# Two passes of scores, their masks and the products with V in one half slot (layer 1 of a two-layer block, TensorE queue)

## The chip, the cores and the metric

The kernel runs on one core of a Trainium2 chip. The metric is the device time of one execution in microseconds. Before the change it is 2129.03 us, the median of three runs (2125.49, 2129.03 and 2129.18 us).

## The reference, cut to what matters

The program is two layers over x of shape (32, 256, 128), that is 32 sequences of 256 tokens. Each layer adds the outputs of an attention-like branch and a mixture of experts to its input. Layer 0 (a Mamba block and eight dense experts) is not touched. In layer 1, for each sequence:

```
q, k, v = up(x @ W_down)                    # 16 heads; q and k of 8 numbers per token, half of them rotated (rope)
scores  = einsum('bhqd,bhkd->bhqk', q, k) / sqrt(8);  causal mask to -inf
att     = softmax(scores);  y = einsum('bhqk,bhkd->bhqd', att, v);  x += y @ Wc
logits  = xn @ wg;  the two best of 128 experts per token, 32 places per expert
x      += g1 * expert(e1) + g2 * expert(e2)
```

## The kernel before, in words

`layer1` writes one queue of instructions per engine, all from the same clock of half slots. `schedule` (L1190 on) counts `now` from -24; a sequence has `HS1 = 12` half slots, and the tables `PE_AT`, `ACT_AT`, `DVE_AT`, `POOL_AT` and `SP_AT` (L1180 to L1184) say in which half slot, counted from the sequence's own start, a step is put into its engine's queue. So in the steady state each queue repeats every 12 half slots, and a step at 24 stands in half slot 0 of a later round. A half slot lasts no fixed time: it only orders the queues, which hold each other back by semaphores. Within one half slot the order is that of the statements in the engine's `half` function. The figures below are half slots modulo 12.

Attention goes over the 16 heads in six units u = 0 to 5. Units 0 and 3 hold four heads (of each half of the rows) with 128 columns each, the others two with 256. A unit passes through these steps:

- **First pass** (`first_pass`, L1358 on; matmuls at L1369 and L1376): scores into PSUM `S1`, and the causal mask added to them by four 64x64 matmuls (`diagonal`, L1355). VectorE then takes the row maxima out of `S1` (L1810). The next unit's first pass waits for that, since `S1` is there once. It stands in the even half slots, 2u.
- The negated maxima of all units are split into three bf16 parts (L1718 to L1724), transposed on TensorE (`nmt`, L1427), copied by ScalarE (`nm`, L1554) and sent by DMA through HBM into rows of `QS`.
- **Second pass** (`second_pass`, L1380 on; L1389 and L1396): transposed scores with the maxima subtracted, into PSUM `S2`, and the mask. ScalarE takes the exponential (L1569) into `PT`. The next unit's second pass waits for that, since `S2` is there once as well. It stands in the odd half slots, 17 + 2u.
- **Products with V** (`values`, L1411 and L1413), in four groups of heads, 128 rows by 9 columns each at four column positions, into PSUM `OT`; two copies (`osb`, L1563) take it away. They come last in their half slots but for `ot`, `yt` and `wc`.

Beside them TensorE has, per sequence: two transposes of normalised rows (`xnt`, L1433), projections for q and k (`qk`, L1439) and their rotated forms (`rot`, L1444), router logits (`g`, L1452), V (`v`, L1457), two running counts of the routing (`count`, L1466 and L1467), the map of places (`map`, L1473), and the epilogue (`ot` L1513, `yt` L1518, `wc` L1523). `xnt`, `qk`, `rot`, `g`, `v` and `nmt` share one PSUM bank `FR`: each waits until the one before it has been read. So `g` waits for VectorE's product `t2` (L1734), which reads what `rot` wrote, and `v` for the top-8 search (`top`, L1739 to L1742), which reads what `g` wrote. The counts share the bank `ACC` in the same way, with ScalarE's copies `cs` (L1550) as readers.

In ScalarE's queue the order within a half slot is xT, v, cs, nm, yT, osb, exp, spl; in VectorE's it is nms, t1, t2, top, mk, loc, oh, add, epi, x, and the maxima last.

The routing runs twice as fast for the first seven sequences (it then has a lead of seven), at one sequence per 12 half slots until it is done, and then the experts run in eight batches, every ten half slots, with indirect DMAs from POOL.

Of the kernel before, what the change touches and what calls it, by code (L numbers as in the profile page):

```python
# [13 lines left out]
P = 128  # L14
# [37 lines left out]
def layer0(nc, ctx, t, dram, scratch):  # L52
# [321 lines left out]
    def _(pe):  # L374
# [93 lines left out]
        def fore(h, n, q):  # L468
            if h == PE_AT["xqt"]:

# [550 lines left out]
GROUPS = 4  # L1021
HG = HEADS // GROUPS
# [6 lines left out]
UNITS = 6  # L1029
# [45 lines left out]
def layer1(nc, ctx, t, dram, scratch, out):  # L1075
# [32 lines left out]
    wc = sb("wc", [P, D])  # L1108
    cos = sb("cos", [P, L]); sin = sb("sin", [P, L])
    maskq = sb("maskq", [P, HG, 64], BF16); maskk = sb("maskk", [P, HG, 64], BF16)  # L1110
# [21 lines left out]
    S1 = ctx.enter_context(nc.psum_tensor("S1", [P, 2, 512], F32))  # L1132
    S2 = ctx.enter_context(nc.psum_tensor("S2", [P, 2, 512], F32))
# [43 lines left out]
    parts_d, nm_d, xn_d, y_d = scratch["parts"], scratch["nm"], scratch["xn"], scratch["y"]  # L1177
    FEW = 4 * J1

    PE_AT = dict(xnt=-21, g=-17, count=(-13, -10), map=-3, qk=-20, rot=-18, v=-3, p1=0, nmt=12, p2=17, pv=(21, 24, 26, 30), ot=(32, 35), yt=36, wc=40)  # L1180
    ACT_AT = dict(xT=-20, cs=(-12, -9), v=-1, spl=(-15, -12), nm=13, exp=18, osb=(26, 32), yT=39)
    DVE_AT = dict(top=-15, mk=-13, loc=(-11, -8), oh=-8, add=-2, t1=-18, t2=-15, mx=1, nms=12, epi=(35, 36), x=43)
    POOL_AT = dict(norm=-23, keep=-13, val=-5, qk=-14, r1=-14, spl=-10)
    SP_AT = dict(xn=-14, parts=(-13, -9, -8), load=-5, nm=12, nm_in=14, we=-16)  # L1184
# [136 lines left out]
    def _(pe):  # L1321
# [26 lines left out]
        def diagonal(scores, mask, heads, off):  # L1348


            for r in range(2):
                for c in range(2):
                    x = 64 * (c ^ r)
                    out = scores[64 * c:64 * c + 64, r, :].rearrange("p (j k) -> p j k", j=heads)[:, :, off + 64 * c:off + 64 * c + 64]
                    last = nc.tensor.matmul(out, identb[x:x + 64, x:x + 64], mask[x:x + 64, 0:heads, :], start=False, stop=True, tile_position=(x, 64 * c))  # L1355
            return last

        def first_pass(u, n, m):  # L1358
            S, a = u // 3, u % 3
            if u == 0:  # L1360
                if n == 0:
                    pe.wait_ge(loaded, LOADED)
                pe.wait_ge(parts_in.sem, parts_in.at(n, 64))
            pe.wait_ge(max_done.sem, max_done.at(n, u))
            if a == 0:
                for j in range(HG):
                    for r in range(2):
                        q, k = QS[rows(r, KQ + 2), m, 4 * S + j, 0:P], KS[rows(r, KQ + 2), m, 4 * S + j, 0:P]
                        nc.tensor.matmul(S1[:, r, j * P:(j + 1) * P], q, k, start=(j == 0), stop=False, tile_position=(64 * r, 0))  # L1369
                last = diagonal(S1, maskq, HG, 0)  # L1370
            else:
                for j in range(2):
                    for r in range(2):
                        i = 4 * S + 2 * (a - 1) + j
                        q, k = QS[rows(r, KQ + 2), m, i, P:L], KS[rows(r, KQ + 2), m, i, :]
                        nc.tensor.matmul(S1[:, r, j * L:(j + 1) * L], q, k, start=(j == 0), stop=False, tile_position=(64 * r, 0))  # L1376
                last = diagonal(S1, maskq, 2, P)
            last.then_inc(p1.sem, 1)

        def second_pass(u, n, m):  # L1380
            S, a = u // 3, u % 3
            if u == 0:
                pe.wait_ge(nm_in.sem, nm_in.at(n, 32))
            pe.wait_ge(exp_done.sem, exp_done.at(n, u))
            if a == 0:
                for j in range(HG):
                    for r in range(2):
                        k, q = KS[rows(r, KQ + 5), m, 4 * S + j, P:L], QS[rows(r, KQ + 5), m, 4 * S + j, P:L]
                        nc.tensor.matmul(S2[:, r, j * P:(j + 1) * P], k, q, start=(j == 0), stop=False, tile_position=(64 * r, 0))  # L1389
                last = diagonal(S2, maskk, HG, 0)  # L1390
            else:
                for j in range(2):
                    for r in range(2):
                        i = 4 * S + 2 * (a - 1) + j
                        k, q = KS[rows(r, KQ + 5), m, i, 0:P], QS[rows(r, KQ + 5), m, i, :]
                        nc.tensor.matmul(S2[:, r, j * L:(j + 1) * L], k, q, start=(j == 0), stop=False, tile_position=(64 * r, 0))  # L1396
                last = diagonal(S2, maskk, 2, 0)
            last.then_inc(p2.sem, 1)

        def values(g, n, m):  # L1400
            S, b = g // 2, g % 2
            if g == 0:
                pe.wait_ge(v_done.sem, v_done.at(n, 1))
                pe.wait_ge(ot_copied.sem, ot_copied.at(n - 1, 2))
            elif g == 2:
                pe.wait_ge(ot_copied.sem, ot_copied.at(n, 1))
            pe.wait_ge(exp_done.sem, exp_done.at(n, 3 * S + b + 2))
            for j in range(HG):
                r, e = j // 2, j % 2
                head, out = 8 * r + 2 * g + e, slice(32 * j, 32 * j + DH + 1)  # L1410
                nc.tensor.matmul(OT[out, b, :], V[m][:, 0, head, :], PT[:, S, 1 + b, 512 * r + L * e:512 * r + L * e + L],  # L1411
                                 start=True, stop=False, tile_position=(0, 32 * j))
                last = nc.tensor.matmul(OT[out, b, P:L], V[m][:, 1, head, :], PT[:, S, 0, 512 * r + P * (2 * b + e):512 * r + P * (2 * b + e + 1)],  # L1413
                                        start=False, stop=True, tile_position=(0, 32 * j))
            last.then_inc(pv.sem, 1)

        def half(due, ahead, now):
            for u in range(UNITS):
                for n, m in due(PE_AT["p1"] + 2 * u):
                    first_pass(u, n, m)  # L1420
                for n, m in due(PE_AT["p2"] + 2 * u):
                    second_pass(u, n, m)
            for n, m in due(PE_AT["nmt"]):
                pe.wait_ge(nm_step.sem, nm_step.at(n, 4))
                front_free("nmt", n)
                for j in range(J1):
                    last = nc.tensor.transpose(FRb[:, j * P:(j + 1) * P], NMS[:, j, :, :].rearrange("p r h -> p (r h)"), identb[:])  # L1427
                last.then_inc(fr_nm.sem, 1)
            for n, m in ahead(PE_AT["xnt"]):
                pe.wait_ge(xn_ready.sem, xn_ready.at(n, 2))  # L1430
                front_free("xnt", n)
                for j in range(J1):
                    last = nc.tensor.transpose(FR[:, j * P:(j + 1) * P], XN[:, m, j, 0:D], ident[:])  # L1433
                last.then_inc(fr_x.sem, 1)
            for n, m in due(PE_AT["qk"]):
                pe.wait_ge(xT_done.sem, xT_done.at(n, 1))
                front_free("qk", n)
                for q, w in enumerate((wq, wk)):
                    last = nc.tensor.matmul(FR[:, q * L:(q + 1) * L], w[:], xnT[:, n % RING, :], start=True, stop=True)  # L1439
                last.then_inc(fr_qk.sem, 1)  # L1440
            for n, m in due(PE_AT["rot"]):
                front_free("rot", n)
                for q, w in enumerate((wqr, wkr)):
                    last = nc.tensor.matmul(FR[:, q * L:(q + 1) * L], w[:], xnT[:, n % RING, :], start=True, stop=True)  # L1444
# [49 lines left out]
            for b in batch(7, now):  # L1494
# [4 lines left out]
                        last = nc.tensor.matmul(ACC[32 * j:32 * j + 32, k * P:(k + 1) * P], XGT[:, k, 32 * j:32 * j + 32], WE[:, b % WBUF, 4 * k + j, :],  # L1499
                                                start=True, stop=True, tile_position=(0, 32 * j))  # L1500
                last.then_inc(applied, 1)
            for g in range(GROUPS):
                for n, m in due(PE_AT["pv"][g]):
                    values(g, n, m)
            for j in range(J1):
                for n, m in due(PE_AT["ot"][j]):
                    if j == 0:
# [400 lines left out]
```

## Time and profile before

| | |
|---|---|
| median of the runs | 2129.03 us |
| profiled execution: span from first to last instruction | 2167.2 us (no other time of it is shown) |
| PE, DVE, ACT, POOL busy | 1941.7, 1681.5, 1340.8, 1310.3 us |
| PE, share of the span | 90% |
| layer 1 | from about 1477 us to the end |
| mean granted TensorE clock | 0.943 of full speed |

The profile is one execution; its engines' rows carry the line of the kernel that issued the instruction. A matmul's end is modelled, so the time from one start to the next is used below rather than its duration. "idle before <-X" names what ended the idle time ahead of an instruction.

### The profile page before, as it was taken

The page shows a single profiled execution, that of the slowest core. Times are in us where ns is not written, and L with a number is a line of the kernel's source. Part 1 is how long each engine was busy: PE and PEld are TensorE (multiplying, and loading weights), DVE is VectorE, ACT ScalarE, POOL GpSimd, SP SyncE. Part 2 cuts the span into 40 slices and gives each one's busy share as a digit, 9 for nine tenths or more (in the row PEclk, how much of TensorE's full clock was granted, in tenths as well). Part 3 has the DMA queues.
Part 4 walks back from the last instruction along what each step waited for, and adds up shares of the span by engine and source line. Part 5 has one row for each costly group of instructions (what it writes and reads, how often), then busy time and mean ns, then how long its engine had stood idle before and what let it go on. Part 6 is the DMA issues. An engine that isn't in the chain of part 4 may idle for free. (4 is left out here: it accounts for less than half of the span.)

```text
span 2167.2 us, 41765 instructions
## 1 busy us (share of the span) xinstructions
PE 1941.7 (90%) x14386; PEld 1129.5 (52%) x14386; DVE 1681.5 (78%) x2731; ACT 1340.8 (62%) x2423; POOL 1310.3 (60%) x1005
## 2 busy tenths in 40 slices
PE   5789999999999999999999999957999999988775
PEld 3455555555555555555555555534555555554442
DVE  5689888888798888887988888857888877774345
ACT  3677676776776777767767777631555555544343
POOL 2586886877867778778687787744433333325430
PEclk7999999999999999999999999976999999998787
DMA  8632633515425335154153362316444444454438
GB/s 205 145 93 56 137 81 80 136 36 124 105 47 134 84 75 138 39 120 112 43 137 84 70 136 66 82 45 174 120 115 123 116 114 116 118 155 129 119 95 239
DMA packets 212029, 235.27 MB, mean 109 GB/s; under 512 B 31590, under 2 KB 150414, under 8 KB 207694
## 3 DMA queue, kind: packets, MB, share of 16 engines
q1 hardware_dynamic: 207116, 227.98, 42.2%
q0 software_dynamic: 2048, 4.18, 0.7%
q8 instruction: 126, 2.06, 0.4%
q14 instruction: 99, 0.81, 0.1%
q10 hardware_dynamic: 2640, 0.24, 0.1%
HBM read 165.51 MB, written 66.85 MB: 107 GB/s over the span
## 5 line engine op out<-in xcount | busy, mean ns | idle before, releaser
L733 POOL TENSOR_TENSOR dBx<-REP,BC 128x1024 f32<-128x1024 f32 x256 | 604.2, 2362 | 260.1 <-DVE dA L906 227.7
L906 DVE TENSOR_TENSOR_SCAN dA<-dA,dBx 128x512 f32<-128x512 f32 x512 | 626.5, 1224 | 151.9 <-POOL dBx L733 105.8
L405 PE MATMUL UP<-xnT,W 128*128 128x512 f32 x1024 | 524.3, 631 | 56.7 <-ACT hT L607 43.4
L414 PEld LDWEIGHTS DN<-W,hT 128*128 128x128 f32 x4096 | 469.3, 192 | 99.4 <-issue 88.2
L414 PE MATMUL DN<-W,hT 128*128 128x128 f32 x4096 | 495.7, 278 | 0.3 <-ACT GD L614 0.3
L598 ACT ACTIVATE dA<-REP,A 128x512 f32<-128x512 f32 x512 | 354.2, 695 | 86.9 <-DVE PR L915 78.7
L607 ACT ACTIVATE hT<-UP,b 128x512 f32<-128x512 f32 x512 | 355.5, 694 | 78.6 <-PE UP L405 70.7
L915 DVE TENSOR_TENSOR PR<-dA,BC 128x512 f32<-128x512 f32 x512 | 353.6, 691 | 33.7 <-DVE dA L906 21.0
L405 PEld LDWEIGHTS UP<-xnT,W 128*128 128x128 f32 x1024 | 180.3, 195 | 296.6 <-issue 150.5
L1810 DVE TENSOR_REDUCE NM<-S 128x4 f32<-128x1024 f32 (+1 forms) x192 | 234.1, 1219 | 128.1 <-PE S L1355 76.8
L1569 ACT ACTIVATE PT<-S 128x1024 f32<-128x1024 f32 x192 | 197.1, 1026 | 124.5 <-PE S L1355 94.5
L614 ACT ACTIVATE GD<-DN,gate 128x128 f32<-128x128 f32 x512 | 145.8, 367 | 129.7 <-PE DN L414 128.5
L743 POOL TENSOR_TENSOR FF<-FF,GD 128x512 f32<-128x512 f32 x128 | 163.2, 1275 | 6.1 <-ACT GD L614 6.1
L426 PE MATMUL YS<-PR,fold 128*32 128x512 f32 x1024 | 141.8, 627 | 1.3 <-DVE y L921 0.7
L1623 POOL TENSOR_TENSOR t<-t 128x512 f32<-128x512 f32 x32 | 40.7, 1272 | 152.6 <-DVE t L1734 152.6
L1411 PE MATMUL OT<-PT,V 128*9 128x256 f32 x1024 | 87.7, 398 | 11.3 <-ACT PT L1569 7.9
L1550 ACT COPY CS<-ACC 128x256 f32<-128x256 f32 x64 | 23.8, 373 | 102.8 <-PE ACC L1467 102.8
L1629 POOL TENSOR_TENSOR SPL<-t,SPL 128x512 bf16<-128x512 f32 x32 | 37.1, 1160 | 79.3 <-ACT SPL L1575 79.3
L1563 ACT COPY OSB<-OT 128x512 f32<-128x512 f32 x64 | 37.5, 586 | 69.7 <-PE OT L1413 57.0
L426 PEld LDWEIGHTS YS<-PR,fold 128*32 128x32 f32 x1024 | 20.6, 110 | 106.8 <-issue 73.1
L972 DVE SCALAR_TENSOR_TENSOR xch<-FRO,convw,xch 128x510 f32<-128x510 f32 (+2 forms) x93 | 69.2, 744 | 8.6 <-ACT xch L657 6.4
L1376 PE MATMUL S<-KS,QS 50*128 50x256 bf16 x512 | 52.8, 285 | 13.4 <-DVE NM L1810 11.0
(251 smaller groups left out, 2667.1 us busy)
## 6 DMA issues: line engine op xcount, KB each, us to landing
BC<-s_b SPq DMA_DIRECT2D x128, 256.0 KB, 6.2
REP<-s_dx SPq DMA_DIRECT2D x124, 256.0 KB, 7.5
REP<-s_delta SPq DMA_DIRECT2D x124, 256.0 KB, 8.8
s_parts<-SPL SPq DMA_DIRECT2D x64, 192.0 KB
KS<-s_parts SPq DMA_DIRECT2D x64, 192.0 KB
QS<-s_parts SPq DMA_DIRECT2D x64, 192.0 KB
s_dx<-tz SPq DMA_DIRECT2D x16, 512.0 KB, 3.1
s_y<-zeros SPq DMA_DIRECT2D x32, 256.0 KB, 2.9
```

What stands on the lines that cost most here:

```text
L405: nc.tensor.matmul(UP[k % 2][:], W1[:, e % E0, f * P:(f + 1) * P], xnT[:, q, :], start=True, stop=True).then_inc(upf.sem, 1)
L414: last = nc.tensor.matmul(DN[:, j * P:(j + 1) * P], hT[:, e % 2, f, j * P:(j + 1) * P], W2[:, e, f, :], start=(f == 0), stop=(f == FB - 1))
L426: last = nc.tensor.matmul(YS[CB * j:CB * j + CB, :], fold[:], PR[:, (DB * b + j) % (2 * DB), :], start=(q == 0), stop=(q == NQ - 1), tile_ ...
L598: nc.scalar.activation(dA[:, k % 3, :], DR[:, h, j, :], ACT.Exp, scale=A[:, h, j, q:q + 1]).then_inc(da_ready.sem, 1)
L607: nc.scalar.activation(hT[:, e % 2, f, :], UP[k % 2][:], ACT.Relu, bias=b1[:, e % E0, f:f + 1]).then_inc(relu_done.sem, 1)
L614: last = nc.scalar.activation(GD[:, e % 2, j, :], DN[:, j * P:(j + 1) * P], ACT.Copy, scale=gate[:, par, j, e:e + 1])
L733: nc.gpsimd.tensor_tensor(dBx[:, s % 2], DX[:, h, j:j + 2, :], BC[:, q // 2, q % 2, :].unsqueeze(1).to_broadcast([P, 2, T0]), ALU.mult).th ...
L743: nc.gpsimd.tensor_tensor(FF[:, par], FF[:, par], GD[:, e % 2], ALU.add).then_inc(acc_done.sem, 1)
L906: nc.vector.tensor_tensor_scan(h, h, dBx[:, k // 2 % 2, k % 2, :], 0.0, ALU.mult, ALU.add).then_inc(scan_done.sem, 1)
L915: nc.vector.tensor_tensor(PR[:, k % (2 * DB), :], dA[:, k % 3, :], BC[:, q // 2, 2 + q % 2, :], ALU.mult).then_inc(prod_done.sem, 1)
L1569: nc.scalar.activation(PT[:, u // 3, u % 3, :], S2[:].rearrange("p b w -> p (b w)"), ACT.Exp, scale=SCALE).then_inc(exp_done.sem, 1)
L1810: nc.vector.tensor_reduce(NM[:, 0 if a == 0 else 1, :].rearrange("p (r i) -> p r i", r=2)[:, :, heads], S1[:].rearrange("p r (j k) -> p r ...
```

## The change

In layer 1 the masks are taken out of `first_pass` and `second_pass` into `first_mask` and `second_mask`, which also carry the signals to VectorE and ScalarE. TensorE's half slot now begins with the scores of both passes, then both masks, then the products with V; all else follows. The second pass moves by one half slot, from 17 + 2u to 18 + 2u, so that it falls into the same even half slots as the first. The exponentials move with it (18 to 19), the products from (21, 24, 26, 30) to (22, 24, 28, 30), and the copies `osb` from (26, 32) to (25, 31). Durations, sizes and numbers of instructions stay.

```diff
-    PE_AT = dict(xnt=-21, g=-17, count=(-13, -10), map=-3, qk=-20, rot=-18, v=-3, p1=0, nmt=12, p2=17, pv=(21, 24, 26, 30), ot=(32, 35), yt=36, wc=40)
-    ACT_AT = dict(xT=-20, cs=(-12, -9), v=-1, spl=(-15, -12), nm=13, exp=18, osb=(26, 32), yT=39)
+    PE_AT = dict(xnt=-21, g=-17, count=(-13, -10), map=-3, qk=-20, rot=-18, v=-3, p1=0, nmt=12, p2=18, pv=(22, 24, 28, 30), ot=(32, 35), yt=36, wc=40)
+    ACT_AT = dict(xT=-20, cs=(-12, -9), v=-1, spl=(-15, -12), nm=13, exp=19, osb=(25, 31), yT=39)
...
-                last = diagonal(S1, maskq, HG, 0)
...
-                last = diagonal(S1, maskq, 2, P)
-            last.then_inc(p1.sem, 1)
+        def first_mask(u):
+            (diagonal(S1, maskq, HG, 0) if u % 3 == 0 else diagonal(S1, maskq, 2, P)).then_inc(p1.sem, 1)
...
+        def second_mask(u):
+            (diagonal(S2, maskk, HG, 0) if u % 3 == 0 else diagonal(S2, maskk, 2, 0)).then_inc(p2.sem, 1)
...
             for u in range(UNITS):
                 for n, m in due(PE_AT["p1"] + 2 * u):
                     first_pass(u, n, m)
+            for u in range(UNITS):
                 for n, m in due(PE_AT["p2"] + 2 * u):
                     second_pass(u, n, m)
+            for u in range(UNITS):
+                for n, m in due(PE_AT["p1"] + 2 * u):
+                    first_mask(u)
+            for u in range(UNITS):
+                for n, m in due(PE_AT["p2"] + 2 * u):
+                    second_mask(u)
+            for g in range(GROUPS):
+                for n, m in due(PE_AT["pv"][g]):
+                    values(g, n, m)
             for n, m in due(PE_AT["nmt"]):
...
-            for g in range(GROUPS):
-                for n, m in due(PE_AT["pv"][g]):
-                    values(g, n, m)
```

TensorE's queue over 12 half slots, after the change (s1, s2 scores, m1, m2 masks, with the unit): 0: s1(0) s2(3) m1 m2 values(1) nmt yt. 2: s1(1) s2(4) m1 m2 count1. 3: xnt. 4: s1(2) s2(5) m1 m2 values(2) qk wc. 6: s1(3) s2(0) m1 m2 values(3) rot. 7: g. 8: s1(4) s2(1) m1 m2 ot0. 9: v map. 10: s1(5) s2(2) m1 m2 values(0). 11: count0 ot1. Half slots 1 and 5 are empty there.

ScalarE's: 0: cs0 spl1. 1: nm osb0 exp(3). 3: cs1 yT exp(4). 4: xT. 5: exp(5). 7: osb1 exp(0). 9: exp(1) spl0. 11: v exp(2). Before, exp(3) stood in 0, exp(4) in 2 behind osb0, exp(5) in 4, exp(0) in 6, exp(1) in 8 and exp(2) in 10.

## Rows read from the trace of the kernel before

**Rows 1.** Windows: busy time (instructions) of PE, PEld, DVE, ACT, POOL; clock, DMA.

```profile
1650.00:1700.00 50.00, 48.34 (x629) 28.96 (x625) 40.17 (x100) 28.28 (x46) 18.22 (x21) 1.00 0.45 119
...
1950.00:2000.00 50.00, 44.06 (x549) 25.14 (x547) 23.68 (x46) 23.96 (x45) 24.51 (x24) 0.83 0.47 130
```

**Rows 2.** Chain that ended last: start, us, what; `qk` of sequences 0, 4, 6, 23.

```profile
1494.34 2.01 PE FR L1439 x4
...
1575.08 1.06 PE FR L1439 x4
...
1616.01 1.06 PE FR L1439 x4
...
1913.02 1.06 PE FR L1439 x4
```

**Rows 3.** Timeline of a steady round: start, us, engine, line, operation, count, [idle].

```profile
1700.69 0.60 PE L1467 MATMUL ACC<-CS,last_row 128*128 128x256 f32 x2
...
1701.33 0.37 ACT L1550 COPY CS<-ACC 128x256 f32<-128x256 f32 x1 [0.40 <-PE ACC L1467]
1701.60 0.38 ACT L1558 COPY yT<-EP 128x256 f32<-128x256 f32 x1
...
1703.51 0.67 PE L1439 MATMUL FR<-xnT,wq 128*128 128x256 f32 x2
...
1704.99 0.40 PE L1389 MATMUL S<-QS,KS 53*128 53x128 bf16 x8
...
1706.11 0.70 PE L1444 MATMUL FR<-xnT,wqr 128*128 128x256 f32 x2
...
1707.17 0.64 PE L1411 MATMUL OT<-PT,V 128*9 128x256 f32 x8
1707.37 0.68 DVE L1734 TENSOR_TENSOR t<-FR,sin 128x512 f32<-128x512 f32 x1
...
1707.96 0.39 PE L1396 MATMUL S<-QS,KS 53*128 53x256 bf16 x4
1708.12 0.59 ACT L1563 COPY OSB<-OT 128x512 f32<-128x512 f32 x1 [1.43 <-PE OT L1413]
...
1708.28 0.25 PE L1355 MATMUL S<-maskk,identb 64*64 64x128 bf16 x4
1708.46 0.71 PE L1452 MATMUL FR<-wvg,xnT 128*128 128x128 f32 x4
1708.61 1.03 ACT L1569 ACTIVATE PT<-S 128x1024 f32<-128x1024 f32 x1
...
1709.21 0.50 DVE L1739 MAX8 mx<-FR 128x8 f32<-128x128 f32 x2 [1.16 <-PE FR L1452]
...
1710.30 1.20 DVE L1810 TENSOR_REDUCE NM<-S 128x4 f32<-128x1024 f32 x1
...
1713.26 1.22 DVE L1810 TENSOR_REDUCE NM<-S 128x4 f32<-128x1024 f32 x1
...
1715.42 0.28 PE L1427 MATMUL FR<-identb,NMS 128*128 128x128 bf16 x2 [0.16 <-DVE NMS L1724]
...
1715.77 0.37 ACT L1554 COPY NMT<-FR 48x256 bf16<-48x256 bf16 x1
...
1716.30 1.22 DVE L1810 TENSOR_REDUCE NM<-S 128x8 f32<-128x1024 f32 x1
...
1717.58 0.39 PE L1376 MATMUL S<-KS,QS 50*128 50x256 bf16 x4 [0.22 <-DVE NM L1810]
```

**Rows 4.** Timeline, earlier, while the routing runs at double pace.

```profile
1581.30 0.68 PE L1452 MATMUL FR<-wvg,xnT 128*128 128x128 f32 x4 [0.58 <-DVE t L1734]
```

**Rows 5.** Waits from 1930 to 2090 us: total us, times, longest us.

```profile
DVE NM L1810 <- remote: 43.9, 11, 6.7
```

**Rows 6.** Timeline, late: a gap on PE, and the projection that follows.

```profile
1983.04 0.22 PE L1355 MATMUL S<-maskq,identb 64*64 64x128 bf16 x1 [1.02 <-issue]
...
1985.44 1.22 PE L1439 MATMUL FR<-xnT,wq 128*128 128x256 f32 x2
```

More of the change, by code:

```diff
@@ L1389, in second_pass @@
                         nc.tensor.matmul(S2[:, r, j * P:(j + 1) * P], k, q, start=(j == 0), stop=False, tile_position=(64 * r, 0))
-                last = diagonal(S2, maskk, HG, 0)
             else:
@@ L1396, in second_pass @@
                         nc.tensor.matmul(S2[:, r, j * L:(j + 1) * L], k, q, start=(j == 0), stop=False, tile_position=(64 * r, 0))
-                last = diagonal(S2, maskk, 2, 0)
-            last.then_inc(p2.sem, 1)
+        def second_mask(u):
+            (diagonal(S2, maskk, HG, 0) if u % 3 == 0 else diagonal(S2, maskk, 2, 0)).then_inc(p2.sem, 1)
         def values(g, n, m):
```

## The prediction

> **What bounds the kernel now.** I read the windows first, to see which engine is full in layer 1, then the chain of waits for the pace of a sequence, then the timeline of one steady round. In the steady part PE is busy 48.34 of 50 us at full clock, VectorE 40.17 and ScalarE 28.28 [rows 1]: TensorE's queue sets the pace. Between the projections of sequences 6 and 23 lie 297.0 us, so a round takes 17.5 us; between 0 and 6 it is 20.3 us, while the routing runs at double pace, and from 23 on rounds are longer and uneven [rows 2, 5]. The reader is to see in the timeline that PE goes from one group to the next almost without waiting, and that PE's busy time holds gaps that no semaphore explains: from a pass of scores to its mask 0.32 us (1707.96 to 1708.28) for 512 columns in two pairs, which at 2.4 GHz are 0.213 us, and from the mask to `g` 0.18 us for 128 columns, 0.053 us [rows 3]. So each change between arrangements (64-row scores, 64x64 masks, 32-column products, whole array) costs 0.11 to 0.13 us.
>
> **What the change removes.** Counting changes of arrangement in TensorE's queue over a round: 38 before (5, 2, 4, 3, 3, 2, 4, 3, 3, 4, 2, 3 by half slot) and 22 after (4, 3, 4, 4, 3, 4 by pair). That is 16 fewer at 0.12 us, 1.9 us of PE time a round; PE alone would need 15.6 us. Neither number of matmuls nor their columns change. Bounds for one saved change: 0 (the cost stays in each group) and 0.127.
> The Trainium skill, page "TensorEngine Tiling (Array Packing)", section "Key Properties", says that changing the tiling mode drains the engine while moving between tiles does not. By that rule the gaps above are drains, and the trace agrees (0.11 and 0.13 us). By that rule alone a round would fall to 15.6 us; that is a rival below.
>
> **What it adds: waits.** Before, one pass stood in each half slot, so PE had the other pass and some projection to do while VectorE or ScalarE read `S1` or `S2`. Afterwards both passes stand at the head of the even half slot, and the odd ones hold little or nothing. I lay one steady round after the change, from the start of the first pass of unit 0 at 0.00, by intervals of [rows 3] between starts.
> 1. Two passes of scores take 0.32 + 0.21 us (the second without a change of arrangement; bound above 0.32), both masks 0.18 + 0.05, and 0.05 more for each mask of four heads: products 1 start at 0.87. These take 0.79 (1707.17 to 1707.96): `nmt` at 1.66.
> 2. ScalarE's half slot 1 is nm, osb0, exp(3), in order. nm starts 0.35 after `nmt` (1715.42 to 1715.77), at 2.01; a copy of this size frees ScalarE after 0.27 (1701.33 to 1701.60), osb after 0.49 (1708.12 to 1708.61); so exp(3) starts at 2.77 and ends at 3.80. Its input was masked already near 0.8. The second pass of unit 4 starts at 3.86 (0.06 for a release, as from 1716.30 + 1.22 to 1717.58), where PE would have come to it near 2.4. First wait: 1.5 us. Before, exp(3) stood ahead of nm and osb0.
> 3. In the next half slots the order is cs1, yT, exp(4), and cs1 waits for `count1`, which now follows both masks. From the second pass, 0.32 + 0.18 + 0.05 + 0.12 (the count's first product, 256 columns) brings L1467 to 4.53; the copy follows 0.64 later (1700.69 to 1701.33), at 5.17; yT and two copies' time put exp(4) at 5.71 and the second pass of unit 5 at 6.80. PE would have been there near 5.7. Second wait: about 1.1 us. The maxima of unit 1 (4.5 to 5.7) are not later than that.
> 4. Scores and masks 0.55, products 2 0.79: `qk` at 8.14; `qk` with `wc` 1.48 (1703.51 to 1704.99): first pass of unit 3 at 9.62. Again 0.87 and 0.79: `rot` at 11.28.
> 5. `g` must wait for t2, since both use `FR`. t2 starts 1.26 after `rot` (1706.11 to 1707.37) and takes 0.68: `g` at 13.30, where `rot` alone would end at 12.3. Third wait: 1.0 us. Before, products 3 and the second pass of unit 1 stood between `rot` and `g`; both have moved ahead of them. That this wait exists when the cover is short is seen earlier in the kernel, where `g` stood 0.58 us for t2 [rows 4].
> 6. `g` to the top-8 search 0.75, from there to the maxima of unit 4 1.09, from these to those of unit 5 2.96 (add, mk and the epilogue lie between), 1.23 and 0.06 to release the next round: 19.39. PE comes there at about 19.2, so VectorE ends the round narrowly.
>
> So a round takes 19.4 us in place of 17.5, PE's saved 1.9 us having turned into idle time: 3.8 us between what PE needs and the round, in the three waits and some smaller ones. Queued behind PE's waiting instruction is all its later work, first masks and maxima among it; that is in the sum. DMAs don't move: SP and POOL keep their places. The load of `QS` and `KS` keeps its lead of five half slots, and the second pass of unit 0, which needs the maxima by DMA, comes 7.6 us after nm (9.62 against 2.01); before it was 6.7 (1715.77 to 1704.99 + 17.5).
>
> **The sum.** Steady: 17 rounds by 1.9 = +32 us (bounds 1.5 and 2.3 a round, as the release and the second pass of scores vary: 26 to 39). First six rounds: in the later ones a round takes 20.5 us (1575.08 to 1616.01, two rounds) [rows 2]; PE has 3.0 us more there, which fills part of the waits, while the double routing adds searches and copies of its own; an estimate of 1.1 each, +7 (bounds 0 and 1.9, 0 to 11). The end, from 1913 us: VectorE alone stood 43.9 us there for something that the trace can't name [rows 5], and these delays don't depend on the order. Without routing the chain above loses the copy cs1 and the wait for t2 before `g`; I take half a microsecond by eight rounds, +4 (0 to 9). Clock: PE would be busy some 80% of a round, about half between 2.2 and 6.8. Late in the trace a gap of 1.02 us was followed by projections at 1.2 GHz: 1.22 us for a wq product where 0.67 is usual [rows 3, 6]. Step 4 holds 2.8 us of PE work on the path, which doubles at worst to add 2 us or a little more. The ends are no fall at all and one in every round, 0 and 34; the rows show only that a gap of this size can do it, so I stay near the lower end: a quarter of the 17 rounds at 2 us, +8. Together 32 + 7 + 4 + 8 = +51 us. The profiled execution spans 2167.2 us, 38 more than the median of the runs; on it this makes 2218, and as the steady rounds are bound by queues and not by the recording I add the same 51 to the median: 2180 us.
>
> **Rivals.**
> - Faster: PE stays the bound and the saved changes pay. For it: PE is at 97% and the gaps are there to be saved. Against it: it needs exp(3) to reach unit 4 before PE does, at 2.4 rather than 3.86, and `g` not to meet t2. It decides at those two places. 23 rounds by 1.9 less and about 5 at the end: 2129 - 49 = 2080 us. Chance 0.12.
> - No change or little: two of the three waits are shorter than laid out, say because copies release sooner or PE's groups shrink more than by 0.12 a change; 1.9 us saved against 2 us waited. 2130 us, 2115 to 2150. Chance 0.12.
> - The clock: with 20% of PE idle the granted clock falls in most rounds, as in the late window, 0.83 at 44 of 50 us busy [rows 1]. Then 17 rounds by 2 us instead of a quarter of them: 2180 + 26 = 2206, 2195 to 2235. Chance 0.20.
> - The change doesn't do what it says: the two passes are queued together but changes cost the same. Then at most 16 by 0.12 come back on the path, 17 rounds by 1.9: 2180 to 2212 us. Its chance is held in the forecast's and the clock's, whose ranges cover it.
>
> **How the numbers follow.** Forecast 2180 us with its own range 2150 to 2205, chance 0.56. Faster rival 0.12, little change 0.12, clock 0.20. From 2130 to 2218 lie the forecast, half of the little-change case and most of the clock's: about 0.8. A measurement of this kernel tells 0.2%, some 4 us, from no change: faster 0.14 (the first rival and a sixth of the second), same 0.05, slower 0.81.
>
> **What would show it.** PE's share in the steady windows falls from 97% to near 80%; the round grows to about 19.4 us. Step 2: the second-pass matmuls at the old L1396 idle about 0.5 us and more on the exponential, once right after osb. Step 3: the same again, with ScalarE waiting for the count. Step 5: `g` idles 1.0 us on t2 once a round. The saving: score to score near 0.21 us without a gap. Wrong would be rounds under 17.5 us, no idle time at `g`, or an exponential that starts ahead of osb0.

## The result, and the profile after

The changed kernel takes 2205.95 us, the median of four runs (2204.43 to 2208.63 us), beside 2129.05 us for the kernel before: a ratio of 1.0374, 95% interval 1.0358 to 1.0391. That is 77 us slower, 26 us above the forecast of 2180: 1 us over the forecast's own range of 2150 to 2205, and inside the 2130 to 2218 that the prediction gave about 0.8. In the kernel after, most of layer 1's lines stand nine to twelve lower: `qk` is L1451, `g` L1464, t2 L1743, the maxima L1819, the exponential L1578, the passes L1369/L1375 (first) and L1390/L1396 (second).

The spans of the two profiled executions, 2167.2 and 2202.6 us, differ by only 35, since the profiled execution of before lay 38 above its own median. Its end is the long part: 254 us from its last projection of [rows 2], against 223 after and 211 to 232 in every other kernel profiled here. So the stages below are compared up to there.

The projections that answer to [rows 2], from the chain of waits of the kernel after (start, us):

```profile
1490.02 2.00 PE FR L1451 x4
...
1578.37 1.06 PE FR L1451 x4
...
1624.20 2.00 PE FR L1451 x4
...
1979.69 1.80 PE FR L1451 x4
```

(In both kernels two projections, of sequences 0 and 1, stand ahead of the first row; the rows called 0, 4, 6 and 23 are of sequences 2, 6, 8 and 25. The intervals are not touched by this. The first projection of layer 1 starts at 1453.3 us in the kernel before, so layer 1 begins earlier than the 1477 us named ahead.) The first six rounds take 134.2 us in place of 121.7, the 17 after them 355.5 in place of 297.0. So 71 of the 77 us are in these 23 rounds.

The window that answers to the first of [rows 1] (busy time and instructions of PE, PEld, DVE, ACT, POOL; clock; DMA), and PE's waits from 1620 to 1920 us, 14 rounds (us in total, times, longest us):

```profile
1650.00:1700.00 50.00, 39.38 (x555) 24.65 (x555) 39.76 (x93) 24.09 (x41) 17.35 (x20) 1.00 0.36 98
```

```profile
PE S L1375 <- DVE NM L1819: 26.3, 40, 1.2
...
PE FR L1464 <- DVE t L1743: 12.2, 14, 0.9
PE S L1396 <- ACT PT L1578: 8.8, 14, 0.7
PE S L1369 <- DVE NM L1819: 7.8, 14, 0.6
```

The reader is to see that PE is busy 79% of the steady window where it was 97%, at full clock, and that in every round it waits four times for maxima, once for t2 and once for an exponential. An undisturbed round is 20.19 us. One of them, from the timeline (start, us, engine, line, operation, count, [idle]):

```profile
1709.08 0.70 PE L1456 MATMUL FR<-xnT,wqr 128*128 128x256 f32 x2
...
1710.24 0.69 DVE L1743 TENSOR_TENSOR t<-FR,sin 128x512 f32<-128x512 f32 x1 [0.71 <-PE FR L1456]
...
1711.08 0.68 PE L1464 MATMUL FR<-wvg,xnT 128*128 128x128 f32 x4 [0.87 <-DVE t L1743]
1711.69 0.39 PE L1375 MATMUL S<-KS,QS 50*128 50x256 bf16 x4
1711.80 0.50 DVE L1748 MAX8 mx<-FR 128x8 f32<-128x128 f32 x2 [0.87 <-PE FR L1464]
1711.92 0.38 PE L1396 MATMUL S<-QS,KS 53*128 53x256 bf16 x4
...
1712.88 1.21 DVE L1819 TENSOR_REDUCE NM<-S 128x4 f32<-128x1024 f32 x1
...
1714.20 1.17 POOL L1635 TENSOR_TENSOR t<-t,SPL 128x512 f32<-128x512 f32 x1 [1.93 <-ACT SPL L1584]
...
1714.39 1.53 DVE L1757 TENSOR_TENSOR MK<-iota,ef 128x512 bf16<-128x512 f32 x1
...
1716.34 1.21 DVE L1819 TENSOR_REDUCE NM<-S 128x4 f32<-128x1024 f32 x1
...
1717.70 0.40 PE L1369 MATMUL S<-KS,QS 50*128 50x128 bf16 x8 [0.56 <-DVE NM L1819]
1717.70 1.16 POOL L1638 TENSOR_TENSOR SPL<-t,SPL 128x512 bf16<-128x512 f32 x1 [0.46 <-ACT SPL L1584]
1717.80 1.11 DVE L1729 TENSOR_TENSOR NR<-NM,NMS 128x32 f32<-128x32 f32 x1
...
1718.59 0.64 PE L1413 MATMUL OT<-PT,V 128*9 128x256 f32 x8
...
1719.41 0.29 PE L1439 MATMUL FR<-identb,NMS 128*128 128x128 bf16 x2
...
1720.00 0.58 ACT L1572 COPY OSB<-OT 128x512 f32<-128x512 f32 x1
...
1720.29 1.22 DVE L1819 TENSOR_REDUCE NM<-S 128x8 f32<-128x1024 f32 x1
1720.48 1.02 ACT L1578 ACTIVATE PT<-S 128x1024 f32<-128x1024 f32 x1
1721.57 0.39 PE L1375 MATMUL S<-KS,QS 50*128 50x256 bf16 x4 [1.23 <-DVE NM L1819]
...
1723.10 0.37 ACT L1559 COPY CS<-ACC 128x256 f32<-128x256 f32 x1 [1.60 <-PE ACC L1479]
...
1723.63 1.04 ACT L1578 ACTIVATE PT<-S 128x1024 f32<-128x1024 f32 x1
1723.69 0.39 PE L1375 MATMUL S<-KS,QS 50*128 50x256 bf16 x4 [0.41 <-DVE NM L1819]
...
1724.73 0.39 PE L1396 MATMUL S<-QS,KS 53*128 53x256 bf16 x4 [0.65 <-ACT PT L1578]
...
1726.07 0.70 PE L1451 MATMUL FR<-xnT,wq 128*128 128x256 f32 x2
...
1727.58 0.40 PE L1369 MATMUL S<-KS,QS 50*128 50x128 bf16 x8
```

Two things are to be seen. PE waits at all the places that the prediction laid by hand, though at the first of them (1721.57) the row names maxima and not an exponential. And two VectorE instructions are longer than before: MK (the mask of the chosen experts), 1.53 us at 1714.39, and NR (the rest of the maxima after their first bf16 part), 1.11 us at 1717.80. Each starts 0.1 to 0.2 us behind a GpSimd instruction (1714.20, 1717.70) and ends only after it. In the kernel before they last (1640 to 1900 us; count | busy us, mean ns of one | idle):

```profile
L1748 DVE TENSOR_TENSOR MK<-iota,ef 128x512 bf16<-128x512 f32 x15 | 10.4, 693 | 0.5
L1720 DVE TENSOR_TENSOR NR<-NM,NMS 128x32 f32<-128x32 f32 x15 | 2.9, 192 | 0.5
```

### The profile page after: what moved, and what is told of

It is laid out like the page before. It is cut to its first block and busy times, and to the rows that moved or that the text cites. A ratio compares the mean times of both kernels' runs of the same rounds, so it can differ in the third digit from the quotient of the medians.

```text
span 2202.6 us, 41765 instructions
## 1 busy us (share of the span) xinstructions
PE 1904.2 (86%) x14386; PEld 1124.4 (51%) x14386; DVE 1717.5 (78%) x2731; ACT 1335.0 (61%) x2423; POOL 1309.3 (59%) x1005
## 5 line engine op out<-in xcount | busy, mean ns | idle before, releaser
L405 PE MATMUL UP<-xnT,W 128*128 128x512 f32 x1024 | 517.5, 623 | 59.3 <-ACT hT L607 44.8
L1819 DVE TENSOR_REDUCE NM<-S 128x4 f32<-128x1024 f32 (+1 forms) x192 | 233.9, 1218 | 82.9 <-PE S L1355 82.7
L1578 ACT ACTIVATE PT<-S 128x1024 f32<-128x1024 f32 x192 | 197.2, 1027 | 88.9 <-PE S L1355 88.6
L1375 PE MATMUL S<-KS,QS 50*128 50x256 bf16 x512 | 54.0, 292 | 51.6 <-DVE NM L1819 51.3
L1647 POOL TENSOR_TENSOR OV<-OH,VAL 128x256 bf16<-128x256 bf16 x32 | 20.2, 630 | 111.4 <-DVE OH L1770 98.8
L1396 PE MATMUL S<-QS,KS 53*128 53x256 bf16 x512 | 53.0, 287 | 24.7 <-ACT PT L1578 24.4
```

The lines of the kernel that those rows point to most:

```text
L405: nc.tensor.matmul(UP[k % 2][:], W1[:, e % E0, f * P:(f + 1) * P], xnT[:, q, :], start=True, stop=True).then_inc(upf.sem, 1)
L1578: nc.scalar.activation(PT[:, u // 3, u % 3, :], S2[:].rearrange("p b w -> p (b w)"), ACT.Exp, scale=SCALE).then_inc(exp_done.sem, 1)
L1819: nc.vector.tensor_reduce(NM[:, 0 if a == 0 else 1, :].rearrange("p (r i) -> p r i", r=2)[:, :, heads], S1[:].rearrange("p r (j k) -> p r ...
```

## The experiments

Round lengths below are from one `qk` to the next in the steady stretch of each profile; "undisturbed" is the value that repeats at full clock. Ratios are to the kernel before, run beside each. Of the tables' lines the diffs show only the entries that differ; what stands behind # in them is a note.

**One cause undone at a time.** First, the products with V back at their old place in the half slot, so that `g` finds cover again (out from ahead of `nmt`, in ahead of `ot`):

```diff
-            for g in range(GROUPS):
-                for n, m in due(PE_AT["pv"][g]):
-                    values(g, n, m)
...
+            for g in range(GROUPS):
+                for n, m in due(PE_AT["pv"][g]):
+                    values(g, n, m)
```

> The changed kernel with the products with V back at their old place in the half slot, behind the projections and counts; all else as changed. Theory (waits): products 3 stand between rot and g again, so g's idle time on t2 (0.87 us a round in the changed kernel) falls under 0.2 us; against that the products of group 1 come behind nmt, which delays osb0 and the exponential of unit 3 by some 0.3 us, and three more changes of arrangement cost 0.3: the round goes from 20.2 to 19.6 to 19.8 us, the time to 2194 to 2200 us. Rival (g's wait is harmless, or another wait takes its place at once): round within 0.1 of 20.2, time 2203 to 2209.

2214.01 us, ratio 1.0428 [1.0406, 1.0450]; undisturbed round 19.98. A miss: `g` no longer waits (the list of PE's waits doesn't hold it), but the second pass now waits 16.7 us in 260 for exponentials, and `nmt` 14.6, for a VectorE cast that has grown to 1.07 us. So the wait for t2 was real, but with it gone the undisturbed round is only 0.2 us shorter, since two others took its place; and MK fell back to 693 ns there, so the 0.2 is not the worth of that wait alone. The time rose all the same, as the lower clock took more of it: the granted clock from 1640 to 1900 us is 0.91, where the changed kernel has 0.95, and the 17 steady rounds take 361.6 us, where they took 355.5.

The copies `osb` back at (26, 32), so that exp(3) no longer stands behind one:

```diff
-osb=(25, 31)
+osb=(26, 32)
```

> The changed kernel with the copies osb back at half slots 26 and 32, so that the exponential of unit 3 stands ahead of osb0 and behind nm only. Theory from the trace after: the second pass of unit 4 would be free 0.5 us earlier, but the first pass of unit 1 ahead of it in the queue waits for the maxima of unit 0 until 3.87 us of the round, so nothing comes of it: round 20.1 to 20.2, time 2202 to 2208 us. Rival (step 2 of the prediction as written: the exponential behind osb0 sets the first wait): 0.5 us less a round, 19.7, time 2194 to 2199 us.

2194.43 us, 1.0332 [1.0312, 1.0352]; undisturbed round 20.20, unchanged. The first pass of unit 1 holds the queue ahead of the second pass of unit 4, and it waits for maxima, not for exp(3). The time fell in part because fewer rounds ran at the lower clock, five of 17 and not eight: the 17 take 349.8 us in place of 355.5. The rest of the 11.5 us lies mostly behind them, where the profile's end takes 211.7 us in place of 223.0; what made that shorter is not shown.

ScalarE's casts for the split of q and k later, so that GpSimd's L1635 and L1638 move off MK and NR:

```diff
-spl=(-15, -12), nm=13
+spl=(-13, -11), nm=13
```

> The changed kernel with ScalarE's two casts spl, which release POOL's r1 and spl subtractions, moved from -15 and -12 to -13 and -11 half slots. Theory: VectorE's MK (1.53 us against 0.69 before) and NR (1.11 against 0.19) are stretched because they run while POOL runs a tensor_tensor; moved, MK falls to 0.7 and NR to 0.2, the maxima of unit 5 come 0.5 us earlier and those of unit 0 0.9 us: round 19.4 to 19.6, time 2191 to 2196 us. Rival (the stretch belongs to these instructions' own operands or to PE's traffic): durations stay at 1.1 and 1.5, time 2203 to 2209 us.

2199.67 us, 1.0342 [1.0315, 1.0369]; undisturbed round 19.66. VectorE's instructions between 1640 and 1900 us, of after and then of this kernel (count | busy us, mean ns of one | idle):

```profile
L1757 DVE TENSOR_TENSOR MK<-iota,ef 128x512 bf16<-128x512 f32 x12 | 18.4, 1531 | 0.4
L1729 DVE TENSOR_TENSOR NR<-NM,NMS 128x32 f32<-128x32 f32 x12 | 13.3, 1109 | 0.4
...
L1727 DVE CAST NMS<-NM 128x32 bf16<-128x32 f32 x12 | 2.2, 181 | 0.4
```

```profile
L1727 DVE CAST NMS<-NM 128x32 bf16<-128x32 f32 x12 | 13.2, 1101 | 0.4
L1757 DVE TENSOR_TENSOR MK<-iota,ef 128x512 bf16<-128x512 f32 x12 | 8.3, 692 | 0.4
...
L1729 DVE TENSOR_TENSOR NR<-NM,NMS 128x32 f32<-128x32 f32 x12 | 2.3, 192 | 0.4
```

MK and NR are back at the 693 and 192 ns of the kernel before: their size was never the matter, only the meeting with GpSimd. The round gained 0.53 us and not both, 1.76: the L1635 that used to meet MK now meets the cast ahead of NR, which starts at 1717.81 and went from 181 to 1101 ns.

```profile
1717.72 1.16 POOL L1635 TENSOR_TENSOR t<-t,SPL 128x512 f32<-128x512 f32 x1 [4.38 <-ACT SPL L1584]
```

Only four of the 17 steady rounds are undisturbed here; the others stand at granted clocks of 0.80 to 0.98, and the 17 take 350.1 us. So the time missed its range, although the durations of MK and NR came out as expected.

ScalarE's second copy of the counts behind exp(4) rather than ahead of it:

```diff
-cs=(-12, -9)
+cs=(-12, -8)
```

> The changed kernel with ScalarE's copy cs1 moved from -9 to -8, so that the exponential of unit 4 no longer stands behind the copy that waits for count1. Theory: the second pass of unit 5 is released by its exponential 0.8 us earlier and then stands ready with the first pass of unit 2: the round loses 0.6 to 0.8 us, 19.4 to 19.6, time 2191 to 2197 us. Rival (the maxima of unit 1 or the copy xT hold PE as long): less than 0.2 a round, time 2202 to 2208 us.

2200.14 us, 1.0355 [1.0337, 1.0373] (five runs, 2182.2 to 2202.2); undisturbed round 19.38, 0.81 less. So step 3's wait stood on the path, as laid. The round came out as expected and the time did not: the profile is of the fastest run, 18 us under the median, at a mean granted clock of 0.947 where the other four have 0.935 to 0.939. In all four kernels the time follows the undisturbed round only in part, since the share of rounds at the lower clock changes as well.

**The two halves of the change apart.** The new order within the half slot, with the old tables; and the old order with the new tables:

```diff
-p2=18, pv=(22, 24, 28, 30)   exp=19, osb=(25, 31)   # order only, on after
+p2=17, pv=(21, 24, 26, 30)   exp=18, osb=(26, 32)
...
-p2=17, pv=(21, 24, 26, 30)   exp=18, osb=(26, 32)   # shift only, on before
+p2=18, pv=(22, 24, 28, 30)   exp=19, osb=(25, 31)
```

> Half of the change alone: the new order of the code (masks split off, products with V behind the masks), with the tables of before, so that the passes still alternate between odd and even half slots. Theory (the waits come from both passes standing in one half slot with ScalarE's copies ahead of the exponentials): the exponentials keep their places, only g stands closer behind rot (a wait of some 0.4 us): round 17.3 to 17.9, time 2122 to 2138 us. Rival (the place of the products with V and of the masks in the queue is what costs): round over 19, time over 2160 us.

> The other half alone: the tables of after (second pass, exponentials, products and osb moved) with the code of before, so that each pass keeps its mask right behind it and the products with V stay last. Theory: the exponentials of units 3 and 4 still stand behind nm, osb0, cs1 and yT, and exp(0) behind osb1: round 19.8 to 20.6, time 2195 to 2225 us. Rival (splitting masks from scores and grouping them is what costs): round 17.3 to 18.2, time 2122 to 2145 us.

Order only: 2159.07 us, 1.0161 [1.0136, 1.0185], round 18.95. Shift only: 2219.88 us, 1.0451 [1.0424, 1.0479], round 20.95. PE's waits of the first, 1640 to 1900 us:

```profile
PE S L1375 <- DVE NM L1819: 7.6, 13, 0.6
PE S L1369 <- DVE NM L1819: 7.3, 13, 0.6
PE ACC L1478 <- DVE MK L1757: 5.9, 14, 0.4
PE FR L1464 <- DVE t L1743: 5.2, 14, 0.4
```

The first was expected at 17.3 to 17.9 us and missed: four waits of about half a microsecond each come from nothing but the place of the products with V and the masks, while MK and NR last 692 and 193 ns. The shift alone costs most, 3.4 us a round; there the second pass waits 22.0 us in 260 for exponentials, and NR is at 1108 ns. Behind the shift, the order gives 0.76 us back (20.95 to 20.19); without it, it costs 1.44.

**All causes undone together.** The three edits of tables (`osb`, casts, count copy), without and with the products at their old place:

> The same without the first edit: products with V stay behind the masks as in the changed kernel; osb, spl and cs1 moved. Theory: g waits 0.9 us for t2 as in the changed kernel, two changes of arrangement fewer: round 17.9 to 18.4, time 2128 to 2150 us. Rival (the wait of g is hidden by other work once the exponentials come early): as e5 or shorter, 17.0 to 17.5.

> The changed kernel with all four edits: products last in the half slot, osb back at 26 and 32, casts spl at -13 and -11, cs1 at -8. Theory: with exp(3) and exp(4) behind nothing that PE still owes, VectorE's two operations short and products between rot and g, a round is laid by the intervals at 17.0 to 17.4 us, held by VectorE's maxima; PE is 90% busy, so the clock stays: time 2105 to 2125 us, at or under the kernel before. Rival (two passes in one half slot cost by themselves, as maxima and exponential of one unit gate the next together): round over 18.2, time over 2140 us.

Without: 2182.34 us, 1.0262 [1.0234, 1.0291], undisturbed round 18.84, most rounds at 19.8 to 20.0. With: 2160.06 us, 1.0156 [1.0125, 1.0188], round 18.24 where 17.0 to 17.4 was expected. The rest is again VectorE beside GpSimd (PE's waits, then VectorE's cast):

```profile
PE S L1375 <- DVE NM L1819: 19.8, 42, 0.7
PE FR L1436 <- DVE NMS L1733: 14.6, 14, 1.0
```

```profile
L1727 DVE CAST NMS<-NM 128x32 bf16<-128x32 f32 x14 | 15.4, 1103 | 0.5
```

So the next kernel moves the first cast once more, and VectorE's searches of the counts behind the maxima that hold up PE:

```diff
-spl=(-13, -11)   loc=(-11, -8)   # on the kernel with all four edits
+spl=(-12, -11)   loc=(-10, -8)
```

> The kernel with all four edits, further the first cast spl at -12 (its subtraction on POOL then runs behind nms instead of beside it) and loc at -10 and -8 (VectorE takes the maxima of unit 0 ahead of the count's read). Theory (with the exponentials early, VectorE's chain from the maxima of unit 5 to those of unit 0 sets the round): the first of the nms casts falls from 1.11 to 0.2 us, the first pass of unit 1 starts 1.3 to 1.6 us earlier, round 16.6 to 17.1 us, time 2105 to 2130 us. Rival (another collision or wait takes the place): round over 17.6, time over 2140 us.

2133.86 us, 1.0044 [1.0028, 1.0059], a little over the range expected; rounds from 16.5 to 18.1, uneven, and one of 19.9 at the lower clock. MK, NR and the casts are all short (692, 192, 181 ns). What PE waits for is now a transfer: between 1640 and 1920 us, 6.6 us at L1390 and 3.4 us at L1369. SyncE's queue shows why: the store of the negated maxima (L1291) is issued at 1711.82, though ScalarE's copy began at 1709.08, because two stores stand ahead of it: that of the normalised rows (L1271, issued at 1709.80), which waits for GpSimd, 109.8 us in that stretch, and that of the first part of q and k (L1260, at 1710.74).

```profile
SPq L1271 <- POOL XN L1641: 109.8, 17, 9.3
...
PE S L1390 <- DMA QS<-s_nm: 6.6, 8, 1.8
...
PE S L1369 <- DMA QS<-s_parts: 3.4, 4, 1.2
```

The last step takes these stores out of the way:

```diff
-SP_AT = dict(xn=-14, parts=(-13, -9, -8), ...
+SP_AT = dict(xn=-7, parts=(-11, -9, -8), ...
```

> e8_maxima_first with SyncE's order changed: the store of the normalised rows (L1271) goes from half slot 10 to 5 of the round and the store of the first part (L1260) from 11 to 1, so that the store of the negated maxima stands behind neither. Theory (what is left of the loss in the steady rounds of e8_maxima_first is TensorE waiting for QS, because its store stood in SyncE's queue behind a store that waits for GpSimd): the 6.6 us that L1390 and the 3.4 us that L1369 wait for the DMAs between 1640 and 1920 us fall under 2 us together, all steady rounds are 16.5 to 17.0 us, and the time falls by 6 to 14 us from 2134, to 2120 to 2128. Rival (the uneven rounds come from the end of GpSimd's chain, splits and XN, and the stores only wait for it): the waits for s_parts grow as those for s_nm go, rounds stay between 16.5 and 18.1 us, and the time stays at 2130 to 2138.

2122.6 us (12 runs) beside 2127.18 (17 runs), ratio 0.9984 [0.9969, 0.9998]: ahead of both kernels by time, though by less than the 0.2% that a measurement here can tell. All 17 steady rounds are 16.48 to 16.50 us. Its window, and the longest of PE's waits there:

```profile
1640.00:1900.00 260.00, 246.31 (x3470) 155.21 (x3471) 217.56 (x552) 155.60 (x251) 84.50 (x108) 1.00 0.47 129
```

```profile
PE S L1375 <- DVE NM L1819: 11.3, 32, 0.4
```

The steady rounds give 17 by 1.02 = 17 us. The first six take 130.6 us in place of 121.7 and give 9 back. That would leave 8 us, where the medians differ by 4.6. An attempt on these:

```diff
-map=-3, qk=-20
+map=-2, qk=-20
```

> e10_sp_order with TensorE's map (L1482) one half slot later, 9 to 10. In the first six rounds of e10_sp_order, where the routing runs at double pace, the map stood twice in two rounds up to 1.44 us (1579.14, 1600.92) because it shares the bank of the counts and had come to stand ahead, by one half slot, of the copy and the searches that read the count before it; right behind the second of these the clock is down (1.22 us for a wq product at 1602.04). Theory (that wait and the clock behind it are a good part of what the first six rounds lose, 130.6 against 121.7 us): the map's wait falls under 0.5 us, the first six rounds to 124 to 128, the steady rounds stay within 16.4 to 16.8, and the time is 2114 to 2121 us. Rival (the first six rounds are held by VectorE, busy 82% there, and by its cast stretched beside GpSimd's L1635; the map's wait is slack): they stay at 129 to 132 us and the time at 2119 to 2127; or the map's sums in VectorE now hold up the maxima behind them and the steady rounds grow by 0.2 us and more.

2169.44 us, 1.0183 [1.0160, 1.0206]: the rival's second half came true. The first six rounds got longer still (134.1 us), 2.7 of the 3.5 us in the first of them, which ran wholly at the lower clock (granted 0.50, against 0.66). The steady ones went from 16.49 to 18.96. VectorE's sum of the map waits 1.17 us for the later map, MK and the maxima of unit 5 stand behind it, and the timeline shows NR beside GpSimd again, at 1.11 us:

```profile
1717.02 0.29 DVE L1776 TENSOR_TENSOR MAP<-MAP,ACC 128x128 f32<-128x128 f32 x1 [1.17 <-PE ACC L1482]
...
1719.98 1.11 DVE L1729 TENSOR_TENSOR NR<-NM,NMS 128x32 f32<-128x32 f32 x1
```

**The clock by itself.** The changed kernel with 18 matmuls of 128 columns more per round, whose results nobody reads, put into PE's idle time (eight ahead of the first pass of unit 1, three ahead of unit 2's, seven ahead of `g`):

```diff
+            for n, m in due(25):
+                pe.wait_ge(ot_copied.sem, ot_copied.at(n, 1))
+                filler(OT[:, 0, 0:P], 8)
+            for n, m in due(31):
+                pe.wait_ge(x_upd.sem, x_upd.at(n - 1, 1))
+                filler(EP[:, 0:P], 7)
...
+            for n, m in due(27):
+                filler(OT[:, 0, 0:P], 3)
```

> The changed kernel with 18 extra 128-column matmuls a round that nothing uses, put where PE waits: 8 ahead of the first pass of unit 1, 3 ahead of that of unit 2, 7 ahead of g. Theory (a part of the loss is the clock, which falls to 1.2 GHz in some rounds because of those idle stretches): the undisturbed round stays at 20.2 (within 0.2), the rounds of 21.7 and 21.9 us go, and the 17 steady rounds last 343 to 348 us in place of 355.5; time 2190 to 2200 us. Rival (the falls have nothing to do with PE's idle time): the long rounds stay, time 2203 us or more.

2193.01 us, 1.0311 [1.0283, 1.0339]. Every steady round is 20.19 to 20.21 us. The windows 1760 to 1780 and 1640 to 1900 us of after, and then the latter of this kernel:

```profile
1760.00:1780.00 20.00, 16.47 (x180) 9.80 (x178) 13.46 (x30) 9.40 (x16) 4.75 (x6) 0.83 0.26 66
...
1640.00:1900.00 260.00, 206.12 (x2731) 126.72 (x2735) 193.34 (x431) 121.94 (x198) 72.51 (x85) 0.95 0.37 100
```

```profile
1640.00:1900.00 260.00, 217.99 (x3063) 141.03 (x3063) 200.95 (x453) 126.76 (x206) 75.36 (x89) 1.00 0.37 102
```

The granted clock goes from 0.95 to 1.00 and the time falls by 13 us: more work, less time. In the 17 steady rounds of the profiles the gain is 12.2 us (355.5 to 343.3), and that is what the clock costs there. The first six rounds gained nothing (134.2 and 136.1 us) and the clock still fell in them; what it costs there and at the end is not measured.

## Why the prediction was right, and where its sizes were off

The direction and the mechanism held, but for one releaser that the text didn't name (step 2 below); the time came out 26 us above. By the steps, counted from the first pass of unit 0 (1717.70, and 1697.51 for those before it, a round of 20.19 earlier):

1. Products at 0.89 (0.87 forecast), `nmt` at 1.71 (1.66). The saving is real: from score to score without a change of arrangement 0.23 us (1711.69 to 1711.92), against 0.32 with one [rows 3]. By the Trainium skill, "TensorEngine Tiling (Array Packing)", section "Key Properties", the mode switch drains the engine and a change of tile doesn't; this trace agrees. PE's own need per round was put at 15.6 us. Busy time gives 15.9 for the changed kernel (39.38 of 50 us in rounds of 20.19) and 15.6 for the kernel with the even rounds (246.31 of 260, 16.49). But by the same measure the kernel before needs 16.9 and not 17.5 (48.34 of 50 [rows 1]), so the saving seen is 1.0 to 1.3 us a round where the text had 1.9.
2. exp(3) starts at 2.78 (2.77). But at 3.87 PE is let go by the maxima of unit 0, a hair later than the exponential (1720.29 + 1.22 against 1720.48 + 1.02 us), and this wait of 1.23 us is the round's longest. The text named one releaser where there were two side by side; taking one away changed nothing (round 20.20). The second pass of unit 4 follows at 4.09 (3.86).
3. exp(4) at 5.93 (5.71), the second pass of unit 5 at 7.03 (6.80), with 0.65 us of wait for it after 0.41 for maxima: 1.06 in sum, forecast 1.1. Moving the count's copy gave 0.81 us back: shown.
4. `qk` 8.37 (8.14), unit 3's first pass 9.88 (9.62), `rot` 11.57 (11.28).
5. `g` at 13.57 (13.30), 0.87 us of wait for t2 (1.0). Shown; with this wait gone, and MK short, the round lost only 0.2.
6. `g` to the search 0.72 (0.75), to the maxima of unit 4 1.08 (1.09), to those of unit 5 **3.46 (2.96)**, to the next round 1.36 (1.29). VectorE ends the round, as said.

The step that fell short is the sum of VectorE's chain in steps 2 and 6: the text took each VectorE duration from [rows 3], where MK and NR met no GpSimd instruction. With the queues shifted against each other, MK took 1.53 us in place of 0.69 and NR 1.11 in place of 0.19. MK's 0.84 covers the 0.50 of step 6; NR stands ahead of the maxima of unit 0 (1717.80 and 1720.29), and its 0.92 more covers the 0.2 to 0.3 by which steps 2 to 5 are late. Together that is the round of 20.19 in place of 19.39. Moving GpSimd's work away brought both back to size and the round down 0.53, while the cast ahead of NR grew by as much as NR had: that the meeting costs time is shown, its full worth of 0.8 us a round only summed.

By terms, with the medians 77 us apart:

| term | forecast (bounds) | measured |
|---|---|---|
| steady, 17 rounds | +32 (26 to 39) | +45.6 (17 by 2.68) |
| clock | +8 (0 to 34) | +12.3 in eight of 17 rounds; 12.2 by the filler kernel |
| first six rounds | +7 (0 to 11) | +12.5 |
| the rest, start and end | +4 (0 to 9) | +6.5, what is left of 77 |

The steady term is outside its bounds, since these varied only the release and the pass of scores. So is that of the first six rounds. Its cause is not settled: in the kernel with even rounds of 16.49 they still take 130.6 us, and the one attempt at them failed. The clock is not all of it, as in two of the six rounds it is full in both kernels and they grew from 21.0 and 21.1 to 22.6 us. What grew most from 1520 to 1615 us are PE's waits of `v` for ScalarE's `xnT` (1.8 to 6.4 us), of `map` for VectorE's search of the count (none to 4.1) and of `g` for t2 (1.4 to 3.5). The rest isn't read from a stage at all, as the end of the profiled execution of before can't stand for its other runs.

The rivals: the clock's 2206 us is the number that came out, but not its reason; the clock took some 12 us in the steady rounds where that case needed 34. "Faster" named exp(3) and `g` as the two places on which it turns. It took more than these: also the count's copy, VectorE's searches, GpSimd's splits and SyncE's stores had to move before PE's saved time could be had, and then it was 1.02 us of the 1.9. That changes "cost the same" is refuted by the 0.23. Of the signs named ahead, PE's share near 80% (79%), `g`'s wait (0.87), the wait behind the count (0.65) and the score gap were there; the wait "once right after osb" was there by place, but put down to maxima.

## What to carry to other kernels

When two producers that took turns are put into one slot, lay each consumer's queue out instruction by instruction: what stands ahead of the release there (a copy, a search, a store that waits for a third engine) may have been free before and be on the path now. A duration copied from the old trace holds only while the same instructions run beside it; look for a second engine whose work slides over it. And a saving on the bounding engine came out here only when the last of such waits went: single repairs moved the undisturbed round by 0 to 0.8 us, and all of them together by 3.7. Read such repairs from the undisturbed round first; the time also holds what the clock took, and it rose by 8 us in one kernel whose round had become shorter.

## What the runs showed of the hardware that was not expected

Three VectorE instructions on 128x32 and 128x512 tiles in SBUF, each begun 0.1 to 0.2 us behind a GpSimd `tensor_tensor` of 1.16 to 1.17 us, ended only after it: NR went from 192 to 1109 ns, MK from 693 to 1531, a cast from 181 to 1101. NR ended 0.05 us behind L1638 (1718.91 and 1718.86), MK 0.55 behind L1635. The maxima, which read PSUM, stay at 1.22 us beside L1638 of the kernel with even rounds. The page "SBUF — State Buffer" of the Trainium skill, section "Who interferes with whom", says that the two engines share a pair of ports and whoever issues first holds it for the whole instruction, and that this concerns VectorE's instructions with two SBUF inputs beside a GpSimd instruction that reads SBUF, and copies and casts in a mode that uses both ports; the trace agrees as far as it goes: the three that grew are of these kinds and the maxima are not. The ports themselves, and the mode of the cast, no run here shows.

The granted clock fell in eight of 17 rounds of the changed kernel although no wait of PE there exceeded 1.23 us and PE was 79% busy in the undisturbed ones; with 18 short matmuls more in the idle time it stayed at 1.00. The kernel with the shift alone kept 1.00 from 1640 to 1900 us as it is, at 210.80 of 260 us busy and with no wait over 0.9 us. Why the same round keeps its clock in some repetitions and not in others stays open.
